# Two layers of attention and feed-forward on one core: the second attention's weighted sums taken once per head pair, a bf16 mask, and a feed-forward order without pass borders

## The reference

```python
# second attention, 4 heads of 64
q, k, v = split(layernorm(x) @ Wqkv + bqkv)
scores = q @ k.T / 8 + graph_bias * adj
scores = where(adj == 0, -1e9, scores)
x = x + (softmax(scores) @ v).heads_together @ Wout + bout
# second feed-forward: h = layernorm(x), then 30 passes of
h = h + 0.01 * tanh(h)
h = h * sigmoid(h)
h = layernorm(h, ln_w, ln_b) @ W.T + b
# out = x + h
```

## Time and profile before

| | |
|---|---|
| runs shown | 3155.28, 3157.41, 3149.43 us; median 3155.28 |
| profiled execution | 3131.73 us, its span in the trace 3130.1 us |
| busy, share of the span | TensorE 87%, VectorE 73%, ScalarE 58%, GpSimd 32% |
| second attention | about 1,640 to 2,340 us |
| second feed-forward | about 2,340 to 3,130 us |

### The profile page before, as it was taken

How to read it: one execution, slowest core, us unless ns; L and a number is a source line. 1 busy time by engine, 2 the same in 40 slices (tenths; PEclk the granted TensorE clock), 3 DMA queues, 4 the chain that set the end, 5 groups by cost and what they waited for, 6 DMA issues and landing times. The chain is left out here.

```text
span 3130.1 us, 57601 instructions
## 1 busy us (share of the span) xinstructions
PE 2720.6 (87%) x19954; PEld 2400.5 (77%) x19955; DVE 2284.0 (73%) x4115; ACT 1813.6 (58%) x3006; POOL 1014.9 (32%) x1575
## 2 busy tenths in 40 slices
PE   7688988999989519983679999999986999999999
PEld 6588888889889519971667777777775888888887
DVE  3699999999999514435557777777767777777776
ACT  2477777777777103321446666666655777777775
POOL 3000000000000251128321121212118788877876
PEclk9878888888888659995889999999997999999999
DMA  5011100000000622222101111110100000000001
GB/s 187 0 36 36 35 35 35 35 35 33 20 35 19 215 83 71 70 64 66 48 5 55 36 43 45 35 53 35 53 6 1 0 0 0 0 0 0 0 0 36
DMA packets 53514, 122.49 MB, mean 39 GB/s; under 512 B 7402, under 2 KB 38734, under 8 KB 47822
## 3 DMA queue, kind: packets, MB, share of 16 engines
q1 hardware_dynamic: 46350, 102.28, 9.5%
q0 software_dynamic: 7104, 19.41, 1.9%
HBM read 97.39 MB, written 24.27 MB: 39 GB/s over the span
## 5 line engine op out<-in xcount | busy, mean ns | idle before, releaser
L1802 PE MATMUL f_pm<-f_wl,f_yt 128*128 128x256 f32 x2640 | 614.2, 381 | 16.7 <-ACT f_yt L1742 16.1
L555 PE MATMUL a_po<-V,a_wt 128*128 128x65 f32 x3872 | 541.6, 309 | 79.0 <-ACT a_wt L428 78.8
L555 PEld LDWEIGHTS a_po<-V,a_wt 128*128 128x128 f32 x3872 | 533.2, 225 | 89.6 <-ACT a_wt L428 89.3
L1802 PEld LDWEIGHTS f_pm<-f_wl,f_yt 128*128 128x128 f32 x2640 | 484.3, 191 | 79.4 <-ACT f_yt L1742 22.8
L115 POOL TENSOR_SCALAR f_yy<-f_th,f_rs 128x255 f32<-128x255 f32 x660 | 366.3, 570 | 21.8 <-POOL f_rs L110 21.8
L1663 DVE SCALAR_TENSOR_TENSOR f_gg<-f_th,f_pm 128x512 f32<-128x512 f32 x319 | 219.3, 688 | 189.7 <-ACT f_th L1752 181.1
L547 PE MATMUL a_tp<-ident,a_lg 128*128 128x128 f32 x1936 | 279.5, 310 | 40.3 <-ACT a_lg L457 38.9
L921 DVE CUSTOM_DVE_ANT_0 a_sc<-a_qk,ADJ 128x1024 f32<-128x1024 f32 (+1 forms) x264 | 288.4, 1093 | 30.7 <-PE a_qk L1019 30.7
L1752 ACT ACTIVATE f_th<-f_pm 128x512 f32<-128x512 f32 x319 | 190.5, 597 | 205.2 <-PE f_pm L1802 205.2
L451 ACT ACTIVATE a_low<-F 128x2708 f32<-128x2708 f32 x88 | 224.9, 2556 | 141.9 <-DVE a_lg L481 138.8
L862 POOL TENSOR_TENSOR ADJ<-ADJ,a_off 128x2708 f32<-128x2708 f32 x22 | 131.2, 5965 | 537.6 <-DVE ADJ L941 537.6
(11 more groups left out here) (234 smaller groups left out, 4620.1 us busy)
## 6 DMA issues: line engine op xcount, KB each, us to landing
ADJ<-in_adj SPq DMA_DIRECT2D x44, 1354.0 KB, 5.8
W<-in_L_ffn_w SPq DMA_DIRECT2D x32, 512.0 KB, 10.1
XD<-p_zeros SPq DMA_DIRECT2D x1, 7680.0 KB
m_rows<-XD SPq DMA_DIRECT2D x60, 128.0 KB, 2.1
YD<-m_y POOLq DMA_DIRECT2D x60, 128.0 KB, 2.0
out<-X SPq DMA_DIRECT2D x21, 128.0 KB
X<-in_x SPq DMA_DIRECT2D x3, 768.0 KB, 9.2
p_wqkv<-in_L_gnn_Wqkv SPq DMA_DIRECT2D x1, 768.0 KB, 4.5
```

The costliest lines, as they stand in the source:

```text
L555: mm = pe.matmul(po[:, b, h * VW:(h + 1) * VW], wt[:, j, :], V[:, j, h, :], start=(j == 0), stop=(j == NT - 1))
L1802: mm = pe.matmul(out, yt[:, g % RING, r, k, :], wl[:, k, :], start=(k == 0), stop=(k == KD - 1))
```

## The change

Four edits, all in the second layer.

1. `weighted` of a pair runs once, after the pair's three chunks, over all 22 tiles (88 instructions), and no longer chunk by chunk behind the transposes. `wt` holds a whole pair in one buffer instead of two buffers of a chunk.
2. `off`, the mask, is bf16 instead of f32. GpSimd's add reads it in that form.
3. MASKED is -2^30 instead of -1e9.
4. In the feed-forward the orders of TensorE, ScalarE and VectorE run on over the border of two passes: the last three products of a pass lie between the first three turns of the next, the last tanh and silu between the next pass's first copies, and the last two statistics behind its first two blends. `yt` has a buffer for each of the 11 groups instead of a ring of four.

```diff
-MASKED = -1e9
+MASKED = -2.0 ** 30
...
-        off = ph.sb("off", [P, N])
+        off = ph.sb("off", [P, N], BF16)
...
-        wt = ph.sb("wt", [P, 2, 2, CT, P])
+        wt = ph.sb("wt", [P, 2, NT, P])
...
-            def weighted(i, b, hp, c):
+            def weighted(i, b, hp):
-                if c == 0 and pair_before(i, b, hp):
+                if pair_before(i, b, hp):
                     pe.wait_ge(heads_out, pairs(*pair_before(i, b, hp)))
-                for g, (j0, end) in enumerate(chunk_groups(c)):
+                for c in range(NC):
+                    for g, (j0, end) in enumerate(chunk_groups(c)):
...
-                    if c:
-                        weighted(i, b, hp, c - 1)
-                    elif pair_before(i, b, hp):
-                        weighted(*pair_before(i, b, hp), NC - 1)
+                weighted(i, b, hp)
...
-        yt = ph.sb("yt", [P, RING, 2, KD, P])
+        yt = ph.sb("yt", [P, NPAIR, 2, KD, P])
...
+        def elementwise_dve(dve, i):
             for g in range(NPAIR):
-                blend(g)
+                blend(dve, i, g)
                 if g >= 2:
-                    stats(g - 2)
-            stats(NPAIR - 2)
-            stats(NPAIR - 1)
+                    stats(dve, i, g - 2)
+                elif some(i):
+                    stats(dve, i - 1, g - 2 + NPAIR)
...
+        def act_stream(act, i):
+            for g in range(NPAIR):
+                if some(i):
+                    turned_out(act, i, g)
+                if g >= LAG:
+                    if not (isinstance(i, int) and i == ITERS):
+                        tanh(act, i, g - LAG)
+                elif some(i):
+                    tanh(act, i - 1, g - LAG + NPAIR)
+                if g >= LAG + 1:
+                    if not (isinstance(i, int) and i == ITERS):
+                        silu(act, i, g - LAG - 1)
+                elif some(i):
+                    silu(act, i - 1, g - LAG - 1 + NPAIR)
...
+        def pe_stream(pe, i):
             for g in range(NPAIR):
+                turn(pe, i, g)
                 if g >= LAG:
+                    product(pe, i, g - LAG)
+                elif some(i - 1):
+                    product(pe, i - 1, g - LAG + NPAIR)
```

More of the change, by code:

```diff
@@ L835, in copy_group @@
             eng.wait_ge(turned[bank(group)], uses(i, b, group))
-            copy(wt[:, (hp * NC + c) % 2, s, j - c * CT:end - c * CT, :],
+            copy(wt[:, s, j:end, :],
                  tp[:, bank(group), 0:(end - j) * P]).then_inc(copied[bank(group)], 1)
@@ L1050, in shares @@
                              ident[:, :]).then_inc(turned[bank(group)], 1)
-            def weighted(i, b, hp, c):
-                if c == 0 and pair_before(i, b, hp):
+            def weighted(i, b, hp):
+                if pair_before(i, b, hp):
                     pe.wait_ge(heads_out, pairs(*pair_before(i, b, hp)))
-                for g, (j0, end) in enumerate(chunk_groups(c)):
[L1057 to L1060, removed]
-                        for s in range(2):
[L1062 to L1066, removed]
+                for c in range(NC):
+                    for g, (j0, end) in enumerate(chunk_groups(c)):
+                        for s in range(2):
+                            group = ("turn", hp, s, c, g)
+                            pe.wait_ge(copied[bank(group)], uses(i, b, group))
+                        for j in range(j0, end):
+                            for s in range(2):
+                                mm = pe.matmul(po[s * HD:(s + 1) * HD, 0:P], V[:, j, 2 * hp + s, 0:HD],
+                                               wt[:, s, j, :],
+                                               start=(j == 0), stop=(j == NT - 1))
+                mm.then_inc(heads_in, 1)
             def project(i, b, k):
@@ L1103, in _ @@
             over_blocks(pe, pair)
-            weighted(NPAIR - 1, 1, HPAIR - 1, NC - 1)
             pe.wait_ge(copied[0], 2 * ROUNDS * NPAIR)
@@ L1657, in _, with blend, stats @@
             sp.wait_ge(stored, NT * 16)
[L1659 to L1675, removed]
+        def blend(dve, i, g):
+            first = isinstance(i, int) and i == 0
+            src = gg[:, g, :, :] if first else pm[:, g % RING, :].rearrange("p (r d) -> p r d", r=2)
+            dve.wait_ge(tanh_done[g], i + 1)
+            dve.scalar_tensor_tensor(gg[:, g, :, :], th[:, g, :, :], 0.01, src, ALU.mult,
+                                     ALU.add).then_inc(g_done[g], 1)
+        def stats(dve, i, g):
+            dve.wait_ge(silu_done[g], i + 1)
+            for r in range(2):
+                dve.bn_stats(st[:, 2 * g + r, :], th[:, g, r, :]).then_inc(stat_done[g], 1)
+            k = batch_of(g)
+            if g == BATCHES[k][1] - 1:
+                a, z = BATCHES[k]
+                for q in range(a, z):
+                    dve.wait_ge(stat_done[q], i * 2 + 2)
+                row_moments(dve, st, mom, 2 * a, 2 * z, folded[k], i * 3).then_inc(moments[k], 1)
+        def elementwise_dve(dve, i):
             for g in range(NPAIR):
-                blend(g)
+                blend(dve, i, g)
                 if g >= 2:
-                    stats(g - 2)
-            stats(NPAIR - 2)
-            stats(NPAIR - 1)
+                    stats(dve, i, g - 2)
+                elif some(i):
+                    stats(dve, i - 1, g - 2 + NPAIR)
         def elementwise_pool(pool, i):
@@ L1729, in _ @@
                                      ALU.add).then_inc(c_done, 1)
-            elementwise_dve(dve, 0, lambda g: gg[:, g, :, :])
+            elementwise_dve(dve, 0)
             with dve.Fori(1, ITERS) as i:
-                elementwise_dve(dve, i, lambda g: pm[:, g % RING, :].rearrange("p (r d) -> p r d", r=2))
+                elementwise_dve(dve, i)
+            stats(dve, ITERS - 1, NPAIR - 2)
+            stats(dve, ITERS - 1, NPAIR - 1)
             for g in range(NPAIR):
@@ L1737, in _, with turned_out @@
                                   X[:, 2 * g:2 * g + 2, :], ALU.add).then_inc(out_done, 1)
[L1739 to L1763, removed]
+        def turned_out(act, i, g):
+            act.wait_ge(turned[g], i)
+            act.copy(yt[:, g, :, :, :], pt[:, g % RING, :]).then_inc(yt_done[g], 1)
@@ new lines, in tanh, with silu @@
+        def tanh(act, i, g):
+            if isinstance(i, int) and i == 0:
+                act.wait_ge(h_done, 2 * g + 2)
+                src = gg[:, g, :, :]
+            else:
+                act.wait_ge(h_mm[g], i)
+                act.wait_ge(y_done[g], i * 2)
+                src = pm[:, g % RING, :]
+            act.activation(th[:, g, :, :], src, ACT.Tanh).then_inc(tanh_done[g], 1)
+        def silu(act, i, g):
+            act.wait_ge(g_done[g], i + 1)
+            act.activation(th[:, g, :, :], gg[:, g, :, :], ACT.Silu).then_inc(silu_done[g], 1)
@@ L1768, in _ @@
             act.copy(wt[:, :, :, :], pt[:, 0, :]).then_inc(w_sb, 1)
-            act_stream(act, 0, True)
-            with act.Fori(1, ITERS) as i:
-                act_stream(act, i, False)
-            for g in range(NPAIR):
[L1773 to L1807, removed]
@@ new lines, in _, with turn @@
+            act_stream(act, 0)
+            act_stream(act, 1)
+            with act.Fori(2, ITERS) as i:
+                act_stream(act, i)
+            act_stream(act, ITERS)
+        def turn(pe, i, g):
+            q, here = last_user(g)
+            pe.wait_ge(y_done[g], i * 2)
+            if here or some(i - 1):
+                pe.wait_ge(yt_done[q], i if here else i - 1)
+            for r in range(2):
+                for k in range(KD):
+                    mm = pe.transpose(pt[:, g % RING, (r * KD + k) * P:(r * KD + k + 1) * P],
+                                      yy[:, g, r, k * P:(k + 1) * P], ident[:, :])
+            mm.then_inc(turned[g], 1)
@@ new lines, in product @@
+        def product(pe, i, g):
+            q, here = last_user(g)
+            pe.wait_ge(yt_done[g], i)
+            if here and isinstance(i, int) and i == ITERS:
+                pe.wait_ge(out_done, q + 1)
+            elif here:
+                pe.wait_ge(g_done[q], i + 1)
+            else:
+                pe.wait_ge(g_done[q], i)
+            for r in range(2):
+                out = pm[:, g % RING, r * D:(r + 1) * D]
+                for k in range(KD):
+                    mm = pe.matmul(out, yt[:, g, r, k, :], wl[:, k, :], start=(k == 0),
+                                   stop=(k == KD - 1))
+            mm.then_inc(h_mm[g], 1)
@@ L1808, in pe_stream @@
+        def pe_stream(pe, i):
+            for g in range(NPAIR):
+                turn(pe, i, g)
                 if g >= LAG:
-                    product(g - LAG)
+                    product(pe, i, g - LAG)
+                elif some(i - 1):
+                    product(pe, i - 1, g - LAG + NPAIR)
         @block.tensor
@@ L1828, in _ @@
             pe.wait_ge(ones_done, 2)
-            pe_stream(pe, 1, False)
+            pe_stream(pe, 1)
```

(6 more changed lines are left out.)

## The result

The changed kernel takes 3273.05 us (median of 4 runs, 3265.58 to 3273.91) against 3154.44 before (4 runs): a ratio of 1.037, 95% interval 1.035 to 1.039. The prediction was 3270.

What follows compares the result with a forecast made beforehand. TensorE and VectorE, almost in step, were taken to bound the second attention's pair hp = 1, and TensorE the feed-forward. +105 +20 +0 -10 = +115 us, added to the median, gave 3270 us, range 3190 to 3325.

Steps and rivals of the forecast that it cites:

- The mechanism: Second attention: VectorE's order does not change, so TensorE idles at the shares and the weighted sums then run behind it.
- The order, +105: Second attention: weighted sums at the pair's end lengthen a block from 31.75 to 36.9 us, +105 us in all.
- The wait at the shares: Second attention, pair hp = 1: TensorE waits about 3 us at L1049 for VectorE's copy.
- The clock, +20: Second attention: TensorE's clock falls behind the new wait and slows the visit to the sums, +20 us, bounds 0 to 68.
- I take 12 falls of 1.7: Second attention: 12 of 20 new waits lower TensorE's clock, each losing about 1.7 us of work.
- The rival with falls in both pairs: Second attention: clock falls in hp = 0 and hp = 1, 40 falls at 2.6 us, 3354 us; chance 0.12.
- The mask, 0: Second attention, off on VectorE: bf16 output keeps its 1.56 us, so 0 us; bounds -16 to +13.
- The feed-forward, -10: Feed-forward: order over pass borders shortens a pass from 24.88 to 24.52 us, gaining 10 us over 29 passes.
- The two waits: Feed-forward: turn(0) and turn(6) each wait 0.38 us for GpSimd, adding 0.76 us a pass.
- the 0.21 us that I added between a load and its transposes: Feed-forward, TensorE: the transpose follows its load by 0.21 us, making the release-to-turn path 8.59 us.
- that case: Second attention: VectorE gets ahead during the long visit, shares reached by 10.3 us, stall under 0.84 us; 3121 us, chance 0.06.
- the 18 us counted for the visits saved: Second attention: four fewer visits to the sums a block, 0.84 us, gain 18 us over 22 blocks if TensorE stays the bound.

Runs made afterwards that it cites:

- the filler: Changed kernel plus 10 more f16 matmuls of 512 columns ahead of the shares in each pair hp = 1, result overwritten: 3235.04 us, ratio 1.028.

## Why the prediction was right

The mechanism was the one foreseen. Two terms of the sum are mis-sized, the clock's by 18 us and the feed-forward's by 7, and the order's is off by 3.

- **The order, +105.** Held. The kernel with the filler, in which the clock stays at 1.00, has blocks 4.7 us longer, where the placing by hand gave 5.1, and 3235.0 - 3133.3 = 102 us in all. The pair hp = 0 came out at 17.97 us (2166.36 to 2184.33), placed at 18.2. The pair hp = 1 without the fall is 36.43 - 17.97 = 18.5, placed at 18.7. The wait at the shares appeared at the instruction named; that it is 2.1 and not 3 us is because 0.64 and 0.45 of it fell at the two turns before.
- **The clock, +20.** Too small: the filler shows 38. The step that failed is "I take 12 falls of 1.7", and of it the number: there were 20, 19 behind the waits in hp = 1 and one in hp = 0. The price of 1.7 was right for 16 of them (the row it was taken from, 3.7 of 5 us at half the clock, is 1.85), and four cost twice as much, which makes 41 us of work at most, against 38 measured. Over the 17 blocks compared it is 38.22 - 36.43 = 1.8 us each. The Trainium skill's "TensorE: Matmul & The Clock Gate", section "HAM oscillation", says that a wait between runs of matmuls can put the clock down each time; its example has waits of 3 to 5 us, and here waits of 2.05 to 2.10 did it 19 times of 20. The length of the wait alone does not decide it in these traces. In the first attention of the kernel before, behind the 19 waits counted in the prediction, stands one of 2.58 us at 930.22 with a granted clock of 1.00 behind it and its 44 instructions in 5.13 us, while those behind a wait of 1.12 us at 620.72 took 8.13. The rival with falls in both pairs did not happen, but for the one fall in hp = 0. Its price of 2.6 a fall has no run behind it.
- **The mask, 0.** Held: 1.56 us, and no change alone. The rate for 16-bit operands in the Trainium skill's "VectorE: DVE Perf Modes", section "The perf-mode tier table", did not come with the bf16 output alone (it would have been 0.8 us).
- **The feed-forward, -10.** The runs show -16.7. The two waits are there, at turn(0) and turn(6), but they cost 24.34 - 23.83 = 0.51 us a pass together and not 0.76. GpSimd was placed rightly: from product(4) at 2888.74 to the second rescaled tile, 2895.95 + 2 x 0.555 = 2897.06, are 8.32 us again. But the 0.21 us that I added between a load and its transposes is not paid by a turn that waited: load and transposes both stand at 2886.08, and turn(0) starts at 2897.21, 0.15 behind the release and not 0.27. That makes a pass of 24.34, not 24.52, and 29 x 0.54 = 15.7 us; the last microsecond is within the scatter. ("By the columns half of that" for a turn should read a quarter, half the instructions of half the columns; the 0.43 is right.)
- **The sum.** 102 + 38 + 0 - 17 = 123 measured, 115 predicted. The clock's cost was too low by 18, the feed-forward's gain by 7 and the order's cost too high by 3, so part of the closeness is errors that cancel. The rest is the base: the sum was added to 3155.3, while the kernel before had a median of 3150 beside the experiments. That the forecast came within 3 us of 3273 is in good part luck; the mechanism and the order's price are not.
- **The rivals.** VectorE does not keep up by itself, but the condition named for that case was right: once off, scale, heads and the projection's add leave the stretch in front of TensorE's waits, the shares are reached at 9.5 us (2024.58 to 2034.09, against the 10.3 asked for), the stall is 0.73 us, under 0.84, and the block falls to 31.24. But the 18 us counted for the visits saved do not come as time: against the same VectorE order chunk by chunk, the gain is 0.14 us a block.

That the clock falls because of the wait was shown by the filler and by the kernels without the wait, in all of which it is 1.00 from 1,680 to 2,270 us. Why one pair early in the stage (the visit at 1740.91, 5.02 us) kept its clock, and why one wait of 1.96 us lowered it and another did not, is open.

## What to carry to other kernels

When two engines run nearly in step, work that one of them does in small pieces is what covers the other's late moments; gathered into one piece it saves its fixed costs and uncovers the waits. Before gathering, place one period of both queues by hand with the durations of the trace, and look at what the second engine can do during the long piece: here two instructions moved there took back 103 of the 140 us lost, and the heads product and the projection's add moved ahead of scores took back the rest. Compare the result with the old grouping under the same new order too: here that was the same time, so the order was worth having and the gathering was not. And an order that has just lost its waits should be asked again which result closes one step too late: one statistic taken a blend earlier gave 14 us, the whole new order 17.

## What the hardware showed that was not expected

- Ten matmuls without use in a wait of 2.1 us made the kernel 38 us faster, since they kept the clock at 2.4 GHz. Waits of 1.77 us in the same stage did not bring the clock down, one of two waits of 1.96 us did, and 19 of 20 waits of 2.1 us, with two shorter ones ahead of each. In the first attention a wait of 2.58 us did not.
- GpSimd's add of 2708 elements takes 5.34 us with one bf16 operand and 5.96 with both in f32.
- The combine stage differed by 24 us between two executions of kernels whose code is the same up to there. What makes the difference is open.
